# A cross-attention stage on one core: two groups' scores in a row, and Strassen's sums in three PSUM banks

## The reference

```python
x = x + cross_attention(layernorm(x), ctx_1024)      # 16 heads of 64
x = x + self_attention(layernorm(x))                 # 16 heads of 32, with a bias by distance
x = x + mixture_of_experts(layernorm(x))             # 8 experts, the best 2 for each row
# cross attention, the part that the change touches:
q, k, v = xn @ Wq.T + bq, ctx @ Wk.T + bk, ctx @ Wv.T + bv
q, k, v = (y.reshape(1, -1, 16, 64).transpose(0, 2, 1, 3) for y in (q, k, v))   # two rows of 512 are one position of 16 heads
attn = softmax(q @ k.T / sqrt(64)); out = attn @ v
```

## Time and profile before

| | before |
|---|---|
| median of 3 runs | 1518.34 us (1516.32 to 1519.26) |
| the profiled execution | 1517.86 us, of it the span 1516.1 us |
| PE busy | 1452.8 us, 96% |
| VectorE busy | 1298.2 us, 86% |
| ScalarE busy | 1254.2 us, 83% |
| GpSimd busy | 951.0 us, 63% |

### The profile page before, as it was taken

The page is one execution under the profiler, slowest core; times in us unless marked ns, Lnnn a source line. Parts: engine busy times, 40 slices in busy tenths (PEclk is TensorE's granted clock), DMA queues, the critical chain, the costliest instruction groups (busy, mean ns, idle before and its releaser), DMA issues.

```text
span 1516.1 us, 47982 instructions
## 1 busy us (share of the span) xinstructions
PE 1452.8 (96%) x17942; PEld 1206.2 (80%) x17942; DVE 1298.2 (86%) x1768; ACT 1254.2 (83%) x3039; POOL 951.0 (63%) x980
## 2 busy tenths in 40 slices
PE   6999999999999999999999999999999887599999
PEld 5788888888888888888888888888888764377776
DVE  6788989888888888898888888888889887788995
ACT  4788888888888888888888888888988875666883
POOL 6586877778687878787777878787878522500000
PEclk9999999999999999999999999999999998699999
DMA  4357555565656565655556565656566578766991
GB/s 187 71 110 143 115 135 133 122 138 117 143 113 139 111 143 112 139 119 134 135 116 143 113 145 111 138 111 145 112 137 130 116 154 223 175 232 241 337 329 46
DMA packets 460175, 220.40 MB, mean 145 GB/s; under 512 B 433856, under 2 KB 440000, under 8 KB 453328
## 3 DMA queue, kind: packets, MB, share of 16 engines
q1 hardware_dynamic: 459680, 218.22, 59.6%
q10 hardware_dynamic: 432, 1.32, 0.3%
HBM read 111.96 MB, written 0.56 MB: 74 GB/s over the span
## 4 chain that ended last, share of the span: by engine, by line
PE 85%; DVE 6%; DMA 3%; ACT 2%; POOL 2%; issue 1%; SPq 0%; DVEq 0%; ACTq 0%; POOLq 0%
PE ps_proj L1626 55%; PE ps_s L1676 9%; PE ps_o L1694 8%; PE ps_proj L1895 6%; PE ps_o L1911 3%; DMA pt_s<-p_s 2%; DVE wsp L1375 2%; PE ps_proj L1655 1%; POOL ctx_s L580 1%; DVE cmax L1163 1%; DVE p_s L1176 1%; PE ps_proj L1911 1%; DMA ctx_f<-ctxt_dram 1%; ACT prob L815 0%; PE ps_o L1596 0%
## 5 line engine op out<-in xcount | busy, mean ns | idle before, releaser
L1626 PE MATMUL ps_proj<-ctx_s,wk_s 128*128 128x256 f16 x4032 | 480.6, 273 | 3.9 <-ACT ps_proj L769 3.6
L1626 PE MATMUL ps_proj<-wv_s,ctx_s 128*128 128x256 f16 x4032 | 480.6, 273 | 1.5 <-ACT ps_proj L771 1.5
L580 POOL TENSOR_TENSOR ctx_s<-t_f,ctx_s 128x512 f16<-128x512 f32 x192 | 265.0, 1390 | 279.9 <-ACT ctx_s L717 279.9
L1626 PEld LDWEIGHTS ps_proj<-ctx_s,wk_s 128*128 128x128 f16 x4032 | 379.9, 98 | 66.4 <-issue 24.3
L1626 PEld LDWEIGHTS ps_proj<-wv_s,ctx_s 128*128 128x128 f16 x4032 | 379.9, 98 | 63.4 <-issue 11.4
L815 ACT ACTIVATE prob<-ps_s,nmax 128x256 f32<-128x256 f32 x776 | 357.1, 476 | 8.3 <-DVE nmax L1170 8.1
L1163 DVE TENSOR_REDUCE cmax<-ps_s 128x4 f32<-128x1024 f32 x194 | 237.5, 1224 | 123.9 <-PE ps_s L1676 123.9
L1176 DVE SCALAR_TENSOR_TENSOR p_s<-prob,p_s 128x1024 f16<-128x1024 f32 x196 | 320.3, 1634 | 0.7 <-ACT p_s L826 0.7
L580 POOL TENSOR_TENSOR ctx_s<-ctx_f,ctx_s 128x512 f16<-128x512 f32 x144 | 215.7, 1498 | 10.3 <-ACT ctx_s L712 5.4
L826 ACT ACTIVATE p_s<-prob 128x1024 f16<-128x1024 f32 x196 | 206.6, 1054 | 6.7
L1694 PE MATMUL ps_o<-v_s,pt_s 128*128 128x64 f16 x4704 | 171.6, 194 | 15.2 <-DMA pt_s<-p_s 15.2
(11 more groups left out here) (235 smaller groups left out, 1800.4 us busy)
## 6 DMA issues: line engine op xcount, KB each, us to landing
ctx_f<-ctxt_dram SPq DMA_DIRECT2D x48, 1024.0 KB, 5.4
wst<-w_dram SPq DMA_DIRECT2D x96, 512.0 KB, 5.5
pt_s<-p_s SPq DMA_TRANSPOSE x408, 3.1
tisa<-tisa_scores SPq DMA_DIRECT2D x12, 256.0 KB, 5.7
w_in_f<-w_in_dram SPq DMA_DIRECT2D x2, 1024.0 KB, 6.2
w_f<-wk_dram SPq DMA_DIRECT2D x2, 512.0 KB, 6.4
ctx_f<-ctxt_dram SPq DMA_DIRECT2D x2, 512.0 KB, 7.8
w_f<-wv_dram SPq DMA_DIRECT2D x1, 1024.0 KB, 11.3
```

The lines of the kernel that those rows point to most:

```text
L580: pool.tensor_tensor(out=low[:, n, :, :], in0=sources[n], in1=high[:, n, :, :], op=ALU.subtract).then_inc(ctx_low, 1)
L1626: ins = pe.matmul(ps_proj[:, bank(h, role), sub * QUARTER:(sub + 1) * QUARTER], lhsT, rhs, start=(fresh and sub == 0 and t == 0 and i == 0 ...
```

## The change

The scores of both groups of a half are issued one behind the other, the first into `ps_s`, the second into `ps_o`; both weighings of a half follow each other too, into the fourth bank of `ps_proj` (`out_bank`). The half's order on TensorE becomes M1, two scores, M5, M6, M2, two weighings, M7, M3, M4. Strassen's sums use three banks: M5 goes into the bank that later takes the u4 sum, and the C22 sum goes to SBUF (`c22_f`). M5's wait is for all four low parts of the half before. On ScalarE the context's high part comes at the head of the half, the seed right behind it, the high part of the sums (`sum_highs`) ahead of the exps, and both groups' p parts are made within the half. VectorE's order follows, with p's low part of the second group right ahead of C22's low part. The last step uses other banks and another order. The diff, cut to its core:

```diff
@@ -199,6 +199,7 @@
         m5_f = sb("m5_f", [P, 2, QUARTER], F32, cross)
+        c22_f = sb("c22_f", [P, 2, QUARTER], F32, cross)
         q_s = [sb(f"q_s{k}", [P, NG, T], F16, cross) for k in range(2)]
...
@@ -349,12 +350,15 @@
-        def score_bank(c, g, head):
-
-            return ps_proj[:, head, :] if isinstance(c, int) and c == LAST and g % 2 else ps_s[:, head, :]
-
-
-
+        def score_banks(c, g):
+
+            if isinstance(c, int) and c == LAST and g >= 2:
+                return (ps_proj[:, 0:2, :], ps_s[:, :, :])[g - 2]
+            return (ps_s[:, :, :], ps_o[:, :, :])[g % 2]
+
+        def out_bank(c, half):
+
+            return ps_o[:, 0, :] if isinstance(c, int) and c == LAST and half else ps_proj[:, 3, :]
...
@@ -374,11 +378,11 @@
-        M1, M5, M6, M2, M7, M3, M4 = (0, 0, 0), (3, 3, 3), (4, 4, 1), (1, 1, 0), (5, 5, 1), (6, 2, 2), (2, 6, 1)
+        M1, M5, M6, M2, M7, M3, M4 = (0, 0, 0), (3, 3, 2), (4, 4, 1), (1, 1, 0), (5, 5, 1), (6, 2, 2), (2, 6, 1)
...
-            return (0, (1, 2)[h], (2, 1)[h], 3)[role]
+            return (0, (1, 2)[h], (2, 1)[h])[role]
...
@@ -399,7 +403,7 @@
-        C11, C22, C12, C21 = (0, 0, 0), (3, 1, 1), (2, 0, 1), (1, 1, 0)
+        C11, C22, C12, C21 = (0, 0, 0), (None, 1, 1), (2, 0, 1), (1, 1, 0)
...
@@ -713,6 +717,9 @@
                     act.activation(ctx_s[odd][0][:, 2, :, :], ctx_f[odd][:, 2:4, QUARTER:CH], ACT.Copy).then_inc(ctx_high, 1)
+
+            def sum_highs(k, odd, half):
+
                 act.wait_ge(t_sum, 4 * k - 1 + half)
...
@@ -777,12 +784,12 @@
                     act.wait_ge(c22_done, g - 2)
-                act.activation(m5_f[:, :, :], half_bank(bank(h, 3)), ACT.Copy).then_inc(m5_done, 1)
+                act.activation(m5_f[:, :, :], half_bank(bank(h, 2)), ACT.Copy).then_inc(m5_done, 1)
...
                 role, i, j = which
-                g, ps = 2 * k + h, half_bank(bank(h, role))
+                g, ps = 2 * k + h, c22_f[:, :, :] if which == C22 else half_bank(bank(h, role))
                 if which == C22:
...
@@ -840,30 +847,32 @@
                         weight_sum_highs(h)
+                    if exists(c, 2):
+                        ctx_highs(c + 2, odd, h)
                     if strassen:
                         seed(c + 1, h)
-                    pc, pg = back(c, 2 * h, 1)
-                    if exists(pc, 0):
-                        p_highs(pc, pg)
                     if exists(c, -1) and h == 0:
...
                         alphas(c, 0)
+                    if exists(c, 2):
+                        sum_highs(c + 2, odd, h)
+                    if exists(c, 0):
+                        exps(c, 2 * h, odd)
                     if strassen:
...
                     if exists(c, 0):
-                        exps(c, 2 * h, odd)
-                    if exists(c, 0):
                         p_highs(c, 2 * h)
-                    if strassen:
-                        block_highs(c + 1, h, C11, 1 - odd)
-                    if exists(c, 2):
-                        ctx_highs(c + 2, odd, h)
                     if exists(c, 0):
...
                     if strassen:
-                        for which in (C22, C12):
-                            block_highs(c + 1, h, which, 1 - odd)
+                        block_highs(c + 1, h, C11, 1 - odd)
+                    if exists(c, 0):
+                        p_highs(c, 2 * h + 1)
+                    if strassen:
+                        block_highs(c + 1, h, C22, 1 - odd)
+                    if strassen:
+                        block_highs(c + 1, h, C12, 1 - odd)
                     if isinstance(c, int) and c == NCH - 2:
...
@@ -1159,8 +1168,7 @@
                 dve.wait_ge(s_done, NG * c + g + 1)
-                ps = ps_proj[:, 0:2, :] if isinstance(c, int) and c == LAST and g % 2 else ps_s[:, :, :]
-                dve.tensor_reduce(cmax[:, g % 2, :], ps.rearrange("p b (r k) -> p (b r) k", r=2), AX,
+                dve.tensor_reduce(cmax[:, g % 2, :], score_banks(c, g).rearrange("p b (r k) -> p (b r) k", r=2), AX,
                                   ALU.max).then_inc(cmax_done, 1)
...
@@ -1208,7 +1216,7 @@
                 dve.wait_ge(unit_done, units_through(g) + 5)
-                dve.tensor_tensor(half_bank(bank(h, 3)), half_bank(bank(h, 1)), m5_f[:, :, :], ALU.add).then_inc(c22_done, 1)
+                dve.tensor_tensor(c22_f[:, :, :], half_bank(bank(h, 1)), m5_f[:, :, :], ALU.add).then_inc(c22_done, 1)
...
@@ -1268,23 +1276,24 @@
                         maxima(c, 2 * h, odd)
-                    pc, pg = back(c, 2 * h, 1)
-                    if exists(pc, 0):
-                        p_lows(pc, pg)
-                    if strassen:
-                        add_u4(c + 1, h)
                     if exists(c, -1):
...
                     if strassen:
-                        add_c22(c + 1, h)
-                        block_lows(c + 1, h, C11, 1 - odd)
+                        add_u4(c + 1, h)
                     if exists(c, 0):
...
                     if strassen:
-                        for which in (C22, C12):
-                            block_lows(c + 1, h, which, 1 - odd)
+                        add_c22(c + 1, h)
+                    if strassen:
+                        block_lows(c + 1, h, C11, 1 - odd)
+                    if exists(c, 0):
+                        p_lows(c, 2 * h + 1)
+                    if strassen:
+                        block_lows(c + 1, h, C22, 1 - odd)
+                    if strassen:
+                        block_lows(c + 1, h, C12, 1 - odd)
                     if isinstance(c, int) and c == LOOP_END + 1:
...
@@ -1293,14 +1302,13 @@
                 block_lows(LAST, 1, C21, LAST % 2)
+                add_o(LAST - 1, 0)
                 maxima(LAST, 0, LAST % 2)
-                p_lows(LAST - 1, 3)
                 maxima(LAST, 1, LAST % 2)
-                add_o(LAST - 1, 0)
                 tisa_scores()
                 p_lows(LAST, 0)
+                maxima(LAST, 2, LAST % 2)
                 add_o(LAST - 1, 1)
-                maxima(LAST, 2, LAST % 2)
                 p_lows(LAST, 1)
...
@@ -1609,7 +1617,7 @@
                 elif m == M5:
-                    pe.wait_ge(block_low, 4 * g - 2 + (2 if isinstance(k, int) and g == 2 else 0))
+                    pe.wait_ge(block_low, 4 * g)
                 elif m == M6:
...
@@ -1659,21 +1667,22 @@
+                last = isinstance(c, int) and c == LAST
                 if g == 0:
-                    pe.wait_ge(block_low, 8 * c + 4)
+                    pe.wait_ge(block_low, 8 if isinstance(c, int) and c == 0 else 8 * c + 4)
                 if isinstance(c, int) and c == 0 and g == 0:
                     pe.wait_ge(q_ready, 1)
-                if isinstance(c, int) and c == LAST and g == 1:
-                    pe.wait_ge(block_low, 8 * LAST + 7)
-                elif isinstance(c, int) and c == LAST and g >= 2:
-                    pe.wait_ge(exp_done, NG * c + g - 1)
-                elif g >= 1 or after(c, -1):
+                if last and g == 2:
+                    pe.wait_ge(block_low, 8 * LAST + 8)
+                elif last and g == 3:
+                    pe.wait_ge(exp_done, NG * LAST + 1)
+                elif g % 2 == 0 and (g or after(c, -1)):
                     pe.wait_ge(exp_done, NG * c + g)
...
                             rows = slice(DK * head, DK * head + DK)
-                            ins = pe.matmul(score_bank(c, g, head)[:, r * HC:(r + 1) * HC], q_s[a][rows, g, r * P:(r + 1) * P],
+                            ins = pe.matmul(score_banks(c, g)[:, head, r * HC:(r + 1) * HC], q_s[a][rows, g, r * P:(r + 1) * P],
                                             k_s[odd][b][rows, g, r * HC:(r + 1) * HC], start=(n == 0), stop=(n == 2))
...
@@ -1682,8 +1691,10 @@
                     pe.wait_ge(block_low, 8 * vc + 8)
-                if vg % 2 == 0 and after(vc, -1):
-                    pe.wait_ge(added, 2 * vc + vg // 2 - 1)
+                if isinstance(vc, int) and vc == LAST and vg == 2:
+                    pe.wait_ge(exp_done, NG * LAST + 2)
+                elif vg % 2 == 0 and (vg or after(vc, -1)):
+                    pe.wait_ge(added, 2 * vc + vg // 2)
                 for head in range(2):
...
@@ -1711,25 +1722,28 @@
-                    for half, before, between, behind in ((0, (M1,), (M5, M6), (M2,)), (1, (), (M7, M3), (M4,))):
-                        g = 2 * h + half
-                        units(*before)
-                        if exists(c, 0):
-                            scores(c, g, odd)
-                        units(*between)
-                        vc, vg = back(c, g, PV_LAG)
+                    def weighted(half):
+                        vc, vg = back(c, 2 * h + half, PV_LAG)
                         if exists(vc, 0):
-                            weigh(vc, vg, odd if g >= PV_LAG else 1 - odd)
-                        units(*behind)
+                            weigh(vc, vg, odd if 2 * h + half >= PV_LAG else 1 - odd)
+
```

(24 more changed lines are left out.)

## The result

The changed kernel takes 1546.97 us (median of 4 runs, 1546.6 to 1548.24), the kernel before beside it 1517.33; the ratio is 1.0193, interval 1.0174 to 1.0212: 29.6 us slower. The forecast was 1548. The profiled execution has a span of 1544.9 us against 1516.1.

A forecast was written before the change was run, and what follows sets the result against it. TensorE was taken to bound the cross-stage loop. From 1517.86 us, less 18.2 for back-to-back scores and 2.0 for the last step, plus 50.6 for stalls, came 1548.3 us; range 1496 to 1571.

The forecast's parts named there:

- The bound and the gain: Cross-stage loop: TensorE sets the pace; scores back to back save 0.38 us a step over 48 steps, 18.2 us.
- The stall: M5 after each step's second half (V) waits for VectorE's late low parts: 1.1 us, 46 times, 50.6 us lost.
- The start: Start-up: the change costs nothing, since scores there come after the projections anyway.
- The last step: Last step: p's low part done a step earlier, third maximum no longer behind add_o; some 2 us back.
- The first, no collision: End of the V half: GpSimd does not meet VectorE's low parts, TensorE keeps the pace; 1497.7 us, chance 0.22.
- The fourth, changes of shape that stay: Score blocks in other banks still cost 0.19 us each, so nothing is gained; 1566 us, chance 0.05.
- The third, more loops: Late chain also delays ScalarE's first exps and C22's sum past M4: another 0.5 us a step, 1571 us, chance 0.09.
- the exclusion: VectorE's p and C22 low parts: operations with two SBUF inputs and GpSimd's SBUF reads exclude each other, 1.06 us more.

The follow-up runs named there:

- run 1: Changed kernel, but C22's low part reads its first input from C12's PSUM bank instead of c22_f (values wrong): 1510.6 us, ratio 0.9950.
- run 2: Changed kernel with C12's high and low parts ahead of C22's on both engines: 1524.37 us, ratio 1.0035.
- run 3: Changed kernel with the sums' high part behind both groups' exps on ScalarE, in step 0's first half only: 1539.47 us, ratio 1.0139.
- run 6: Changed kernel with the C22 sum in the first bank of ps_o and step 0's first sums' high part behind the exps: 1503.42 us, ratio 0.9887.
- run 4: Changed kernel with p's low part of each half's second group moved to the head of the next half on VectorE: 1606.04 us, ratio 1.0585.

## Why the prediction was right, point by point

**The bound and the gain.** Right in kind and size. TensorE set the pace, a score block between units costs 0.19 us more than its matmuls, and with two blocks a step freed of this it takes 24.21 (run 1), against 24.22. One reading was a little too strong: the waits of the kernel before also have 24 weight loads that wait 0.21 us for k_s's low part (VectorE). They cost nothing extra, M5 at 704.57 in the earlier trace rows starts the usual 0.76 us after the scores.

**The stall.** Right in place and cause: K's M5, once a step, behind the V half's low parts, with C22's at 1.76 us in V and 0.68 in K; run 1 shows the cause by taking it away, run 2 by making it smaller (0.32 us). The term was too large, 1.1 us for 0.81 (25.03 less 24.22). Two entries of the working account for it. p's second low part was ready at 707.29, 0.17 ahead of the 11.35 us into the half that I had (V's M1 starts at 696.11), and waited 0.37 for GpSimd, not 0.75: GpSimd's sums had begun at 705.28, 9.2 us into the half, against 9.6. Over 46 steps the term came to some 37 us, not 50.6, and the loop to 20.3 lost instead of 32.4; 37.3 less the gain of 18.7 leaves 18.6, and where the other 1.7 lie is open.

**The start.** Wrong. "Start-up: nothing" was decided from the place of the scores alone. Seed and exps had been given a new neighbour, the sums' high part, and I had weighed that wait in the steady loop, where GpSimd is ahead by a little (2.2 us into the half against 2.5); in step 0 it isn't, and run 3 prices the omission at 7.4 us of the 10.1 that K's half of step 0 takes longer than before. Of the 2.7 left in run 3, 1.2 are idle stretches that are longer than in the kernel before (M7's for u4 above all), and 1.5 are M7, M3 and M4 at the lower granted clock. The other 0.4 of the 10.5 lie ahead of step 0, in a part that the change leaves alone; in the nine profiled executions K's M1 of step 0 starts anywhere from 45.0 to 46.3 us.

**The last step.** The 2 us forecast are seen in the sum behind the last mark, but only 0.3 of them in the cross stage (from the last step's first scores to its last weighing 24.00 us against 1262.31 - 1238.05 = 24.26 before, the stretch of the earlier trace rows); the rest lies in later stages, which the change doesn't touch, and which took 251.7 to 253.8 us in the nine profiled executions (253.8 in that of the kernel before, 252.0 in that of the changed one). So the term was too large by 1.7 us, and that the sum behind the mark shows 2.0 is luck.

So the total of 1548 for 1547 owes something to chance: the loop was forecast 12 us too slow, the start 10 us too fast.

**The rivals.** The first, no collision, is the kernel of run 1, but for the start: with both gone (run 6) it is at 1503.4 us, 15.5 faster than the kernel before beside it (1518.9) where the rival had 20. The fourth, changes of shape that stay, is out by the 48 gaps for 97. The third, more loops, did not come in this kernel; run 4 shows how close it lay.

**The page.** The Trainium skill, SBUF — State Buffer, section "Who interferes with whom", gives the exclusion that the forecast rested on; this case's 1758 ns against 684 ns for one and the same operation agree with it.

## What to carry to other kernels

Moving a sum from PSUM to SBUF to save a bank can make the operations that read it collide with GpSimd; count the SBUF inputs of each VectorE operation ahead of a wait, and look up what GpSimd does at that moment in both halves of the loop. Slack has to be read for everything that is queued behind a late operation and for every wait that counts it, not for its nearest reader alone, and a wait that is covered in the steady loop must be checked again in the first step. If a bank is needed, ask first which one stands idle at that moment: the second scores' bank was free for just the stretch in which the sum lived.

## What the runs showed of the hardware

Two VectorE operations with two SBUF inputs that stand next to each other do not keep GpSimd out between them: GpSimd's waiting instruction gets in, and the second operation takes 1.76 us instead of 0.68, every one of the 24 times counted (1755 to 1762 ns). With one operation of 0.6 us that has a PSUM input set between them, the second takes 1.15. The wait is part of the length that the profile gives for the VectorE operation, so it is seen in no list of waits and only as a longer mean of one shape. Even the nmax operation of 128x4 elements, 0.16 us alone, took up to 0.95 us in the loop of the changed kernel.

Behind 8.7 us without a matmul in step 0 TensorE's granted clock was 0.50, the 1.2 GHz level, and 36 matmuls took 6.2 us instead of 4.1; in run 3 the same matmuls took 5.6 us behind an idle stretch of 1.95. So a wait in step 0 cost more than its own length.
